# Unsplit fp32 probabilities as the stationary operand of the value product

## The reference, cut to what matters

```python
k = (context @ Wk).reshape(B, Nk, h, dh)
v = (context @ Wv).reshape(B, Nk, h, dh)
scores = einsum('bqhd,bkhd->bhqk', q, k) * scale
attn = softmax(scores, axis=-1)
out = einsum('bhqk,bkhd->bqhd', attn, v).reshape(B, Nq, h * dh)
return out @ Wo + bo
```

## Time and profile before

| | us |
|---|---|
| median of 3 runs (4688.74 to 4704.13) | 4696.32 |
| the profiled execution | 4716.16 |
| its span, first to last instruction | 4714.4 |
| PE busy | 3969.0 (84%) |
| DVE busy | 3658.0 (78%) |
| ACT busy | 2850.1 (60%) |
| POOL busy | 1046.6 (22%) |
| mean granted clock | 0.849 of 2.4 GHz |

### The profile page before, as it was taken

One profiled execution on the slowest core, in us unless ns is written; L12 is line 12 of the kernel. 1 busy time (PEld: TensorE's weight loads), 2 busy tenths in 40 slices (PEclk: granted clock), 3 DMA queues, 4 the chain that ended last, 5 costly groups with the idle time before them and its releaser, 6 DMA issues. The chain is left out here.

```text
span 4714.4 us, 105294 instructions
## 1 busy us (share of the span) xinstructions
PE 3969.0 (84%) x38240; PEld 2143.3 (45%) x38240; DVE 3658.0 (78%) x15825; ACT 2850.1 (60%) x9049; POOL 1046.6 (22%) x1207
## 2 busy tenths in 40 slices
PE   4767777648999999999999999999588988898759
PEld 2333343334545445445454454544255555555436
DVE  4787888778888888887888888886678888887541
ACT  2555555535666666666666666667177777777712
POOL 1000000000000000000000000000288878888700
PEclk7555555557999999999999999999599999999969
DMA  2222222100000000000000000000312221222020
GB/s 62 66 70 70 68 70 70 60 3 3 2 4 4 2 4 2 3 4 2 3 2 3 3 2 3 2 2 3 93 39 71 73 73 42 67 72 58 3 57 5
DMA packets 97822, 146.85 MB, mean 31 GB/s; under 512 B 14077, under 2 KB 90549, under 8 KB 92150
## 3 DMA queue, kind: packets, MB, share of 16 engines
q1 hardware_dynamic: 97302, 140.13, 10.7%
HBM read 82.32 MB, written 56.56 MB: 29 GB/s over the span
## 5 line engine op out<-in xcount | busy, mean ns | idle before, releaser
L1270 PEld LDWEIGHTS G<-st,rec_w 128*128 128x128 f16 x19456 | 609.9, 100 | 894.7 <-DVE st L1430 854.6
L1664 POOL TENSOR_TENSOR plt<-pft,pht 128x512 f16<-128x512 f32 x765 | 875.2, 1169 | 244.2 <-DVE pht L1891 163.8
L1270 PE MATMUL G<-st,rec_w 128*128 128x1 f16 x19456 | 684.3, 165 | 286.9 <-DVE st L1430 268.8
L1222 PE MATMUL OA<-pf,vals 128*97 128x512 f32 (+1 forms) x1632 | 855.3, 605 | 0.7
L1166 ACT ACTIVATE st<-hb 32x16 f16<-32x16 f32 x1216 | 259.0, 213 | 704.0 <-DVE hb L1425 703.3
L267 DVE TENSOR_REDUCE mx<-MT 128x1 f32<-128x512 f32 (+1 forms) x832 | 520.9, 661 | 96.0 <-PE MT L1710 92.2
L1659 ACT ACTIVATE pft<-ST,ln_prob 128x512 f32<-128x512 f32 (+1 forms) x816 | 541.0, 687 | 64.1 <-PE ST L1732 63.5
L267 DVE TENSOR_REDUCE mx<-MB 128x1 f32<-128x512 f32 (+1 forms) x832 | 537.4, 660 | 48.2 <-PE MB L259 33.5
L1146 ACT ACTIVATE pf<-SC,ln_prob 128x512 f32<-128x512 f32 (+1 forms) x816 | 560.7, 687 | 20.5
L1657 ACT ACTIVATE pht<-ST,ln_prob 128x512 f16<-128x512 f32 x510 | 350.9, 688 | 264.4 <-PE ST L1732 259.0
L1157 ACT ACTIVATE tf<-G 32x16 f32<-32x16 f32 x1216 | 213.0, 175 | 366.3 <-PE G L1270 338.0
(11 more groups left out here) (321 smaller groups left out, 7484.2 us busy)
## 6 DMA issues: line engine op xcount, KB each, us to landing
vc<-scr_v SPq DMA_DIRECT2D x16, 1644.8 KB, 15.9
kc<-scr_k SPq DMA_DIRECT2D x32, 816.0 KB, 13.1
scr_v<-v_hl SPq DMA_DIRECT2D x24, 1032.0 KB, 5.6
scr_k<-k_hl SPq DMA_DIRECT2D x192, 128.0 KB, 1.7
k<-scr_k SPq DMA_DIRECT2D x16, 816.0 KB, 6.7
w<-in_L_ffn_W SPq DMA_DIRECT2D x16, 256.0 KB, 5.8
xin<-x SPq DMA_DIRECT2D x38, 48.0 KB, 1.8
scr_v<-v_hl SPq DMA_DIRECT2D x2, 774.0 KB, 5.7
```

Source lines behind the costliest of these rows:

```text
L1222: pe.matmul(OA[0:at.DC + 1, :], at.vals[0:rows, i, :], pf[0:rows, tile % 2, :], start=(i == 0), stop=(i == KT - 1)).then_inc(pv_done, 1)
L1270: mm = pe.matmul(g[:, t, c:c + 1], rec_w[:, c, :], st[:, c:c + 1], start=False, stop=(c == C - 1), skip_group_check=True)
L1664: return eng.tensor_tensor(pl[0:k, t % NP_, :], pf[0:k, t % NP_, :], ph[0:k, t % NP_, :], ALU.subtract)
```

## The change

Names ahead of the diff: `MB` are two banks that serve the unit work in turn; the `Timetable` hands them out with `take`.

- The recurrence's value product swaps its operands: four fp32 matmuls a tile (`pe_values`), each with 128 queries of one head as stationary and the 97 columns of `vals` moving. The sums lie as 128 x (4 x 97). At a unit's end they are turned back (`pe_flip`, two steps after the unit's end, copied by ACT in two halves) and projected four steps after it; DVE takes the reciprocals straight from `o_sb` and adds the heads two a step. `pe_den` is gone.
- In the tail `ph`, `pl` and all that makes them are gone: one exponential a tile, four fp32 matmuls with `pf` as stationary and 65 fp32 columns of `vc` moving. A head's sums fill one bank, and two banks alternate. The scores of tile t + 3 follow the value product.
- Values per head are stored in fp32 (65 x 4 bytes where 129 x 2 were), without the subtraction on DVE, through the banks `MB`. Keys and values get lists of places of their own: 11 and 11 in a chunk.

```diff
 class Timetable
-        self.out = {start[u] + period: u for u in range(units - 1)}
+        self.flip = {start[u] + period + 2: u for u in range(units - 1)}
+        self.out = {start[u] + period + 4: u for u in range(units - 1)}
...
-        special = {s: 1.3 for s in self.out}
+        special = {s + 1 + i: 0.7 for s in self.out for i in range(2)}
...
 class ByHead
-    PLACES = (0, 1, 2, 3, 4, 5, 7, 8, 11, 12, 13, 14, 15, 18, 19, 20, 21, 25, 28, 30, 31)
+    KEY_PLACES = (0, 1, 2, 4, 7, 8, 15, 18, 21, 25, 31)
+    VALUE_PLACES = (3, 5, 6, 11, 12, 14, 19, 20, 23, 24, 28)
...
-def pe_den(pe, at, bank):
+def pe_values(pe, at, bank, probs, rows, j, last):
+    W = at.DC + 1
     for i in range(at.HEADS_A_UNIT):
-        mm = pe.matmul(bank[:, i:i + 1], at.o_sb[:, i * P:(i + 1) * P], at.pick_den[:, :], start=True, stop=True)
+        mm = pe.matmul(bank[:, i * W:(i + 1) * W], probs[0:rows, i * P:(i + 1) * P], at.vals[0:rows, j, :],
+                       start=(j == 0 and i == 0), stop=last, skip_group_check=True)
     return mm
+def pe_flip(pe, at, bank):
+    for i in range(at.HEADS_A_UNIT):
+        mm = pe.transpose(bank[0:at.DC, i * P:(i + 1) * P], at.o_sb[:, i, 0:at.DC], at.identa[:, :])
+    return mm
...
 tile_values in chunks (PE)
-                        pe.matmul(OA[0:at.DC + 1, :], at.vals[0:rows, i, :], pf[0:rows, tile % 2, :], start=(i == 0),
-                                  stop=(i == KT - 1)).then_inc(pv_done, 1)
+                        pe_values(pe, at, OA, pf[:, tile % 2, :], rows, i, i == KT - 1).then_inc(pv_done, 1)
...
 chunks (ACT)
+                        for half in range(2):
+                            if step - 1 - half in plan.flip:
+                                bank, n = plan.uses["flip", plan.flip[step - 1 - half]]
+                                cols = slice(half * 2 * P, (half + 1) * 2 * P)
+                                a.wait_ge(mb_full[bank], n + 1)
+                                s.activation(at.o_t[:, cols], MB[bank][0:at.DC, cols],
+                                             ACT.Copy).then_inc(mb_read[bank] if half else o_turned, 1)
...
+                                s.activation(v_st[:, half, :, j % by_head.TILES_A_STORE, 0:at.DHEAD],
+                                             MB[i % 2][:, :].rearrange("p (h d) -> p h d", d=at.DHEAD),
+                                             ACT.Copy).then_inc(v_kept, 1)
...
 chunks (DVE)
-                                else:
-                                    _, _, hi, low, product = value_parts(by_head, i)
-                                    v.tensor_tensor(low, product, hi, ALU.subtract).then_inc(k_low, 1)
...
+                        if step in plan.flip:
+                            u = plan.flip[step]
+                            dve.wait_ge(o_kept, u + 1)
+                            v.reciprocal(at.rden[:, :], at.o_sb[:, :, at.DC]).then_inc(r_den, 1)
...
 attention_tail
-    VC = 2 * DHEAD + 1
+    VC = DHEAD + 1
-        vc = sb("vc", [P, 2, KT, VC], F16)
+        vc = sb("vc", [P, 2, KT, VC])
...
-                    if not hi_by_vector(t):
-                        s.activation(ph[0:k, t % NP_, :], SC[t % NS][0:k, :], ACT.Exp, scale=1.0 / at.S_SCALE,
-                                     bias=at.ln_prob[0:k, 0:1])
...
-                for t in range(TOTAL):
-                    if not low_by_vector(t):
-                        pool.wait_ge(p_done, t + 1)
...
-                        low_part(nc.gpsimd, t).then_inc(l_pool, 1)
...
                     for i in range(NB):
-                        if j == 0 and g and i % 2 == 0:
-                            pe.wait_ge(o_free, 2 * g - 1 + i // 2)
-                        pe.matmul(OA[i // 2][:, (i % 2) * 256:(i % 2) * 256 + VC], ph[0:k, t % NP_, i * P:(i + 1) * P],
-                                  vc[0:k, g % 2, j, :], start=(j == 0 and i % 2 == 0), stop=False, skip_group_check=True)
+                        mm = pe.matmul(OA[g % 2][:, i * VC:(i + 1) * VC], pf[0:k, t % NP_, i * P:(i + 1) * P],
+                                       vc[0:k, g % 2, j, :], start=(j == 0 and i == 0), stop=(j == KT - 1),
+                                       skip_group_check=True)
+                    mm.then_inc(pv_done, 1)
                     if t + NS < TOTAL:
                         scores(t + NS)
-                    if low_by_vector(t):
-                        pe.wait_ge(l_dve, low_done(t))
-                    else:
-                        pe.wait_ge(l_pool, t + 1 - low_done(t))
-                    for i in range(NB):
-                        mm = pe.matmul(OA[i // 2][:, (i % 2) * 256:(i % 2) * 256 + DHEAD + 1], pl[0:k, t % NP_, i * P:(i + 1) * P],
-                                       vc[0:k, g % 2, j, 0:DHEAD + 1], start=False, stop=(j == KT - 1), skip_group_check=True)
-                    mm.then_inc(pv_done, 1)
...
 keep_sums (DVE)
-                    for c in range(2):
-                        pair = OA[c][:, :].rearrange("p (a c) -> p a c", a=2)
-                        v.tensor_copy(o_low[:, 2 * c:2 * c + 2, :], pair[:, :, DHEAD:VC]).then_inc(o_lo, 1)
...
+                    v.tensor_copy(o_n[:, :, :], OA[g % 2][:, 0:NB * VC].rearrange("p (a c) -> p a c", a=NB)).then_inc(o_free, 1)
...
-                    if t + 1 < TOTAL and hi_by_vector(t + 1):
-                        dve.wait_ge(p_done, t + 2)
-                        v.tensor_copy(ph[0:k1, (t + 1) % NP_, :], pf[0:k1, (t + 1) % NP_, :]).then_inc(h_dve, 1)
```

More of the change, by code:

```diff
@@ L157, in _ @@
                 pool.memset(at.neg_half[:, :], -0.5)
[L158 removed]
+                pool.memset(at.o_sb[:, :, :], 1.0)
                 pool.memset(at.qh[:, :, :], 0.0)
@@ L305, in dve_q_low, with dve_heads_out @@
     return at.nc.vector.tensor_tensor(at.ql[:, unit, :], bank[0:at.DC, :], at.qh[0:at.DC, unit, :], ALU.subtract)
-def dve_heads_out(dve, at, bank, y, y_step, done, bank_read):
+def dve_heads_out(dve, at, bank, y, y_step, unit, heads, bank_read):
     v = at.nc.vector
-    for i in range(at.HEADS_A_UNIT):
+    done = (at.HEADS_A_UNIT - 1) * unit
+    for i in heads:
         head = bank[:, i * P:(i + 1) * P]
@@ L406, in __init__ @@
         for s in range(steps):
+            if s in self.flip:
+                take(("flip", self.flip[s]), s + 2.3)
             if s in self.out:
-                take(("den", self.out[s]), s + 0.5)
-                take(("out", self.out[s]), s + 0.6)
+                take(("out", self.out[s]), s + 2.6)
             if s in self.turn:
@@ L442, in __init__, with at_places @@
                        for j in range(j0, min(j0 + self.TILES_A_STORE, at.KT))]
-        self.n_keys, self.total = len(self.keys), len(self.keys) + len(self.values)
         self.v_stores = 2 * -(-at.KT // self.TILES_A_STORE)
-        places = [c * chunk_steps + p for c in range(chunks) for p in self.PLACES]
-        assert self.total <= len(places)
-        self.at_step = {s: i for i, s in enumerate(places[:self.total])}
-    def in_chunk(self, chunk, late):
-        return [i for s, i in self.at_step.items()
-                if s // self.chunk_steps == chunk and (s % self.chunk_steps >= self.T_STORE) == late]
+        def at_places(places, n):
+            steps = [c * chunk_steps + p for c in range(chunks) for p in places]
+            assert n <= len(steps)
+            return {s: i for i, s in enumerate(steps[:n])}
+        self.key_at = at_places(self.KEY_PLACES, len(self.keys))
+        self.value_at = at_places(self.VALUE_PLACES, len(self.values))
+    def in_chunk(self, chunk, late):
+        for t in range(self.T_STORE if late else 0, self.chunk_steps if late else self.T_STORE):
+            s = chunk * self.chunk_steps + t
+            if s in self.key_at:
+                yield "key", self.key_at[s]
+            if s in self.value_at:
+                yield "value", self.value_at[s]
 def slstm_stage(nc, x, w, scratch_in, scratch_out, dims, at, first_row, xa_out, keys_out, values_out):
@@ L1279, in _ @@
                             beside(t, p, p + 1)
[L1280 to L1281 removed]
+                            if by_head and n in by_head.key_at:
+                                i = by_head.key_at[n]
                                 if i >= 2:
                                     pe.wait_ge(k_low, i - 1)
[L1284 to L1299 removed]
@@ new lines, in _ @@
+                                pair, a0, a1 = by_head.keys[i]
+                                cols = slice(pair * P, (pair + 1) * P)
+                                out = SC[i % 2][:, 0:a1 - a0]
+                                pe.matmul(out, at.wk_l[:, cols], at.keys_h[0:at.DC, a0:a1], start=True, stop=False)
+                                pe.matmul(out, at.wk_h[:, cols], at.keys_l[:, a0:a1], start=False, stop=False)
+                                pe.matmul(out, at.wk_h[:, cols], at.keys_h[0:at.DC, a0:a1], start=False,
+                                          stop=True).then_inc(k_full, 1)
@@ new lines, in _ @@
```

(11 more changed lines are left out.)

211 lines of the change are left out of this document (78 added, 133 removed).

## The result

The changed kernel takes 4930.75 us (median of 4 runs, 4922.44 to 4957.31) where the kernel before takes 4694.93 (4 runs, 4688.74 to 4704.13): 1.0503 of its time, 95% interval 1.046 to 1.0545. It is slower by 236 us; the forecast was 154, so the sign and the range held and the size was 81 us short. The profiled execution is the longest of the four, 4957.31 us, as the profiled one of before, 4716.16, was; the prediction's sum for a profiled execution, 4870, was 87 short of it.

What follows compares the result with a forecast made beforehand. Bounds: step chain in chunks 0 to 9, nearly PE in 10 to 37, making f16 parts in the tail. Profiled 4716 + 204 - 35 - 15 = 4870 us; median 20 lower, 4850; range 4770 to 4965.

Steps and rivals of the forecast that it cites:

- The price of the product: Recurrence and tail: fp32 matmuls with 128 stationary columns start 0.112 us apart, a tile's value product 0.865 and 0.839 us.
- The third rival: Tail: the load hides behind the stream, 0.055 us at best between instructions, whole kernel 4519 us; chance 0.06.
- the fourth: Recurrence: projection, turns and more PE instructions make steps late, +0.05 us a step, +45 us, 4895 us; chance 0.06.
- The rule of the Trainium skill: Value product: about 81 ns spacing at 128 columns, an estimated 4670 us for the whole; weighed but not followed.
- The new bound in the tail: Tail: PE becomes the bound instead of making the f16 parts, a head takes 78.9 us, +204 us.
- Chunks 0 to 9: First ten chunks: 102 subtractions leave DVE, 3.5 us saved a chunk, -35 us; bounds 20 to 45 us.
- The unit's end: Chunks 10 to 37: about -1 us at each of 15 units' ends, -15 us; the 3.70 us step falls to some 2.4.
- The value product costs PE 0.865 for 0.86 us: Chunks 10 to 37: the new product adds nothing on PE; bounds 0 to +0.03 us a tile, 24 us.
- I keep the share of low clock of before: Tail: mean clock stays at 0.98, 4% of the time at 1.2 GHz, so 1249 us become 1274.
- the sum at 2.4 GHz throughout (1249): Tail: sixteen heads make 1262 us, less 13 us for work the last heads don't have, 1249.
- The rival "the clock falls more often": Tail: short streams leave a fifth of its time at 1.2 GHz, 114 us more, 4964 us; chance 0.12.
- The rival "the clock stays high": Chunks 10 to 37 and tail: calmer units' ends keep 2.4 GHz, 53 and 25 us less, 4772 us; chance 0.10.

Runs made afterwards that it cites:

- kernel 4: Changed kernel with the old tail and value storage (f16 parts, subtractions, two products) put back, recurrence and piece places kept: 4752.4 us, ratio 1.0125.
- kernel 8: Kernel before with only the unit's end spread over five steps and separate key and value places, values through banks MB: 4686.63 us, ratio 0.9974.
- kernel 1: Changed kernel with the recurrence's old value product and denominators and no turn; unit's-end order, pieces and tail as changed: 4882.33 us, ratio 1.0391.
- Kernel 5: Changed kernel with 128 moving columns in the recurrence's value product and, in the tail, for the first head alone: 4855.56 us, ratio 1.0326.

## Why the prediction was right in sign and short in size

- *The price of the product: right.* 0.84 and 0.87 us a tile against 0.839 and 0.865. The distance taken from groups with 1 and with 128 moving columns held for 65 and 97 columns and in the tail's rhythm. One detail of the sum was misplaced without changing it: the short distance of a group (0.056 us, the stream of 65 columns) is the first, not that of the last instruction. The third rival (the load hides behind the stream, faster) is out: seven of a group's eight distances are 0.11 us, not under 0.083, and halving the load halved them. So is the fourth (the recurrence late by its own instructions): away from the units' ends, steps at 2.4 GHz are as long as before. The rule of the Trainium skill weighed in the prediction ("TensorE: Matmul & The Clock Gate", section "Back-to-back issue gap", about 81 ns) is not this case's number. The section "LDWEIGHTS (loading the stationary operand)" of the same page of the Trainium skill divides the columns by 1.2, an estimate of 107 ns for 128 and 53 ns for 64. The runs have 112 and 58 ns at 2.4 GHz, so these fp32 rows agree with that section there; at 1.2 GHz they have 213 ns for 128, and the measurement decides.
- *The new bound in the tail: right.* PE busy 1237 of 1238 us, POOL at zero, a head of 80.1 us for 78.9. The 1.2 us a head that the sum lacks have no single place. Split by the distances from start to start, the sixth head has 43.3 us of value products (42.8 in the sum), 22.5 of scores (22.1), 11.0 of maxima (10.9) and 3.3 for row, turn, projection and queries (3.1).
- *Chunks 0 to 9: right*, -32 for -35, and kernel 4 shows the cause.
- *The unit's end: right.* The one unit's end that ran at 2.4 GHz throughout both before and after the change got shorter by 1.2 us where I had 1, and the step after a unit's last tile takes 2.3 us (median at 2.4 GHz) where it took 3.7. Its order alone is worth 25 us (kernel 8), and there the time at 1.2 GHz falls as well, from 131 to 81 us.
- *The clock: wrong, and most of the miss.* The step that failed is in chunks 10 to 37: "The value product costs PE 0.865 for 0.86 us", "nothing". That holds at 2.4 GHz alone. Under the new product the clock stayed low for longer, 193 us more at 1.2 GHz than with the old one (269 against 76 in kernel 1). For the tail the prediction says "I keep the share of low clock of before". There both ends were off: after its start it never fell (1.00 instead of 0.98, about 25 us less than forecast), and at its start it stayed low for 62 us (28 us more). The two nearly cancel: over the whole tail the mean clock was 0.976 for the 0.98 I had kept, right in size by luck and wrong in its place. The tail's 1295 exceed the sum at 2.4 GHz throughout (1249) by 46 us: 28 for the first head, 18 for about 1.2 us in each of the others. In the recurrence the new product cost 73 us of steps 384 to 1215 (2238.2 against 2165.0 in kernel 1; 48 by the medians of the two kernels), half of it in the first unit (169.0 against 132.9) and half at the low clock of later units; less the 25 us of the unit's end these are the +48 of the table. Kernel 5 takes both away by widening alone and comes to 4855.56 us. That this is 5 us from the forecast is partly luck: the 25 us that I had put down for a low clock in the tail stand for the 1.2 us a head that I had not.
- *The rival "the clock falls more often" had the cause and not the place.* It named the streaming in half of an instruction's time and set it in the tail's whole length. The tail's body was safe; what suffered were the places where the clock had to rise from 1.2 GHz under this product: the first tiles, the units' ends and the tail's start (and, for 3 to 24 us, the middle of a unit here and there). The sentence against it, "the tail loses its idle time for POOL", took idle time for what holds the clock down. The row from 1080 to 1180 with 99.94 of 100 us busy and a clock of 0.50 says otherwise. In the Trainium skill, "TensorE: Matmul & The Clock Gate", section "HAM oscillation — how this bites in real kernels", it is idle gaps of PE that bring the clock down. This trace has no such gap in that stretch, and the clock didn't rise.
- *The rival "the clock stays high" was not what happened after the change*, and its price was set too high. It took 132 x 0.4 = 53 us for the chunks; with its own steps of 3.4 and 2.4 us it is 132 x (3.4 - 2.4) / 3.4 = 39 us. Kernel 1 against the changed kernel has 193 us less at 1.2 GHz and is 73 us shorter there, 0.38 us for each.

What I had not asked of the trace of before: not how often the clock falls, but under which instructions it had risen, at 1118 and at the tail's start, and whether these were still there.

## What to carry to other kernels

Price a product with many stationary loads by its distance from start to start, measured on any group of the same type and stationary width in the old trace; it carried over to within 1%. Then look at each place where TensorE's clock stood at 1.2 GHz and rose, and at whether the instructions it rose under are still there; here 31 more moving columns in the recurrence and 63 in the tail's first head gave back 75 us. And take a change apart: its two reorderings, with value places chosen anew, made the kernel 0.4% faster, while the new arithmetic that came with them cost 5%.

## What the runs showed of the hardware

- PE was busy 99.94 of 100 us at 1.2 GHz with 97 moving columns at 128 loaded ones in fp32, in one profile of the changed kernel; the same product with 128 moving columns stood at 0.97 over the same 100 us, and with 65 moving columns at 64 loaded ones the tail's start had 0.94.
- In the recurrence the clock's first rise came 13.6 to 99.5 us after the first tile in five profiles with 97 moving columns and within 5.0 us in the six others; it fell in the middle of a unit in each of the five and in none of the six. In the tail it came 61 to 62 us after the first value product in four profiles with 65 moving columns at 128 loaded ones, each time 1.0 to 1.9 us after two fp32 instructions of 512 moving columns.
- Once at 2.4 GHz, the tail's stream with the same product kept it for 1238 us (1.00).
- From start to start an fp32 instruction in a group takes 0.112 us for 128 stationary columns and 0.058 for 64 at 2.4 GHz, and 0.213 for 128 at 1.2 GHz. Only the first distance of a group is shorter at 128 stationary columns: 0.056 us with 65 moving ones, 0.086 with 97.
- Groups of 64 stationary columns between groups of 128 cost 0.24 us a round beyond their loads and streams: their first load starts 0.31 us after the matmul ahead has started, where it starts with it when both have 128. What makes it is open.
